# Strassen FFN on one core: the sums of G's blocks on GpSimd instead of DVE

## The chip, the cores and the metric

One core of a Trainium2 chip runs the whole kernel. The metric is the device time in microseconds (us), the median over runs. The core has TensorE (PE, matrix products), ScalarE (ACT), VectorE (DVE), GpSimd (POOL) and SyncE (SP), which issues all DMAs of this kernel.

## The reference

A low-rank mixture layer, then a linear layer whose output is masked, then a residual. `x` is 8 x 256 x 1024, 2048 tokens in all.

```python
# first layer: base + low-rank part, 8 experts of rank 16, top 2 by a router
base = x @ W.T                                       # 1024 x 1024
gates = softmax over the top 2 of (x @ Wr.T + language bias)
y = base + 2 * einsum(x @ A.T, gates, B)
# second layer, masked by hits of a softmax over 64 centroids
dots = softmax(y @ centroids.T / 0.1)
hits = dots > 0.01
query_sel, cluster_sel = any(hits, axis=1), any(hits, axis=0)
out = where(query_sel & cluster_sel[assignments], y @ weight.T + bias, 0)
return x + out
```

## The kernel before

The two linear layers have nothing nonlinear between them, so the kernel first makes G = W' V' (the product of both weights, and of W with the centroids), and then multiplies x by G, with the low-rank part added. Every matrix product is made in three passes over a high and a low part of each operand (`three`, L925): ScalarE copies a tile to the rounded type (`copy`, L393), and DVE subtracts that from the tile to get the low part (`rest`, L581).

**First sweep** (about 10 to 58 us): nine products of a weight block with half of V and the centroids, `m` = 0 to 8. ScalarE evicts each to `gop_raw` or `gb3_raw` and to the centroid columns.

**Second sweep** (about 58 to 187 us): for each pair of token tiles `n` = 0 to 7 TensorE does, in this order: `chunk(n, 0)`, half of the rest of G's row block n; `token_product(0, n)`, the tokens with the low-rank A, the router and the centroids; for `n >= 1` `turn_hg(n - 1)`, which turns the gated low-rank values; `chunk(n, 1)`; `lora_logits(n - 1)`, the low-rank part of the centroid logits, which waits for `hgt_lo` (semaphore `hgt_split`); `token_product(1, n)`. The last two chunks (`chunk(KD, 0)` and `chunk(KD, 1)`) follow.

**Product stage** (from 187 us): x times G, by a Strassen-like scheme. G is cut in 2 x 2 half-size blocks. `gop_raw` has seven slots: R11, R21, R22 (three blocks as they are) and T1 to T4, sums of them. The evictions write R11, R21, R22 and, into slot T3, the block R12. For each of four row blocks `jj`, and for each of the two column ranges (A1 = 224 columns from the first sweep, 288 from the second), four subtractions make T1 = R12 - R11, T3 = R22 - R12 (in place), T2 = R22 - T1 and T4 = T2 - R21. This is `t_sums` (L601), on DVE, eight calls: `k` = 0 to 3 in the first sweep after `m` = 2, 4, 6, 8; `k` = 4, 5, 6 in the second sweep at `n` = 2, 4, 6; `k` = 7 behind the loop over the pairs. Each waits for the eviction of the last block it reads (`g_evicted`); the calls at `n` = 2, 4, 6 and the last one read what `evict(n - 1, 1)` wrote, that is the evictions of n = 1, 3, 5, 7. Within a call T3 and T2 wait for T1, and T4 waits for both, over `t_step`; the last subtraction signals `t_made`.

Who reads the sums: `r_part` (L412) on ScalarE copies the three R slots and waits for the eviction only. `r_rest` (L612) on DVE writes the low part of the R slots into the same memory as their raw values, so it waits for `t_made` and for `r_part`. `t_part` (L417) on ScalarE copies all four T slots of a row block, and waits for `t_made`; `t_rest` (L617) on DVE follows it.

DVE's order is written out by hand. For a pair n in the second sweep (L739 to L752): `split_x(0, n)`, `route(n - 1)`; then for even n `t_sums` and `r_rest`, for odd n >= 3 `t_rest`; then `split_x(1, n)` (`xt_lo`), `split_hgt(n - 1)` (`hgt_lo`), `split_w`, and the softmax of the logits. GpSimd makes five constants at the start and has nothing else to do; it issues no DMA.

Of the kernel before, what the change touches and what calls it, by code (L numbers as in the profile page):

```python
# [5 lines left out]
ALU = mybir.AluOpType  # L6
# [9 lines left out]
HALF = 512  # L16
# [9 lines left out]
KD = D // P  # L26
KO = O // P
KG = KD + 1
KH = KD // 2
# [4 lines left out]
A1 = (HALF - C) // 2  # L34
# [5 lines left out]
R11, R21, R22, T1, T2, T3, T4 = range(7)  # L40
# [12 lines left out]
def adaln_ffn_kernel(nc, x, xt, ids, w9, awt, v1, v2, bias, assign, out):  # L53
# [9 lines left out]
    with ExitStack() as ctx:  # L63
# [3 lines left out]
        def sb_split(name, shape, stack=ctx):  # L67

            with nc.sbuf_tensor(name + "_raw", shape, F32) as raw:
                pass  # L70
            return raw, sb(name + "_lo", shape, F32R, stack)

        def sem(name):
            return ctx.enter_context(nc.semaphore(name))
# [39 lines left out]
        gop_raw, gop_lo = sb_split("gop", [P, 7, KH, HALF])  # L114
# [84 lines left out]
        g_evicted = sem("g_evicted")  # L199
        cent_split = sem("cent_split")  # L200
        t_step = sem("t_step")
        t_made = sem("t_made")
# [63 lines left out]
        def chunk_number(n, c):  # L266
            return KG + 2 * n + c + 1
# [103 lines left out]
        def _(pool):  # L371
# [7 lines left out]
                           allow_small_or_imprecise_dtypes=True).then_inc(const_ready, 1)  # L379
            nc.gpsimd.memset(ones_b[:], 1.0).then_inc(const_ready, 1)  # L380

        def raw_of(kb, cols):

            at = slice(R11, T3 + 1, T3) if kb % 2 == 0 else slice(R21, R22 + 1)
            return gop_raw[:, at, kb // 2, cols]
# [192 lines left out]
        def _(dve):  # L578
            def rest(dst, src, hi):

                return nc.vector.tensor_tensor(dst, src, hi.bitcast(F32), ALU.subtract)  # L581

            def minus(dst, a, b):
                return nc.vector.tensor_tensor(dst, a, b, ALU.subtract)

            def split_w(q):
                b = q % 2
                dve.wait_ge(w_hi_done, q + 1)
                rest(w_lo[b][:], (wraw if q <= KG else w_in_place)[b][:], w_hi[b][:]).then_inc(w_split, 1)
# [6 lines left out]
            def split_v2(p):  # L596
                dve.wait_ge(v2_hi, p + 1)
                j = slice(JP * p, JP * p + JP)
                rest(vt2_lo[:, j, :], vt2_raw[:, j, :], vt2_hi[:, j, :]).then_inc(v2_split, 1)

            def t_sums(k, jj, cols, number):  # L601

                g = gop_raw[:, :, jj, cols]
                dve.wait_ge(g_evicted, number)
                minus(g[:, T1, :], g[:, T3, :], g[:, R11, :]).then_inc(t_step, 1)
                dve.wait_ge(t_step, 3 * k + 1)
                minus(g[:, T3, :], g[:, R22, :], g[:, T3, :]).then_inc(t_step, 1)
                minus(g[:, T2, :], g[:, R22, :], g[:, T1, :]).then_inc(t_step, 1)
                dve.wait_ge(t_step, 3 * k + 3)
                minus(g[:, T4, :], g[:, T2, :], g[:, R21, :]).then_inc(t_made, 1)  # L610

            def r_rest(k, jj, cols):  # L612
                dve.wait_ge(t_made, k + 1)
                dve.wait_ge(r_hi, k + 1)
                rest(gop_lo[:, 0:3, jj, cols], gop_raw[:, 0:3, jj, cols], gop_hi_r[:, :, jj, cols]).then_inc(gop_split, 1)

            def t_rest(jj):  # L617
                dve.wait_ge(t_hi, jj + 1)
                rest(gop_lo[:, T1:T4 + 1, jj, :], gop_raw[:, T1:T4 + 1, jj, :], gop_hi_t[:, :, jj, :]).then_inc(gop_split, 1)
# [12 lines left out]
            def split_x(c, n):  # L632
                dve.wait_ge(xt_hi_done[c], n + 1)
                rest(xt_lo[c][:], xt_raw[c][:], xt_hi[c][:]).then_inc(xt_split[c], 1)

            def set_up():
                dve.wait_ge(const_ready, 5)
                dve.wait_ge(ids_landed, 16)
                dve.wait_ge(assign_landed, 16)
                nc.vector.memset(hit_sum[:], 0.0).then_inc(setup_step, 1)  # L640
                nc.vector.tensor_tensor(lang_bias[:], ids_raw[:].unsqueeze(2).broadcast_to([P, NB, E]),
                                        iota8[:].unsqueeze(1).broadcast_to([P, NB, E]),
                                        ALU.is_equal).then_inc(setup_step, 1)

                nc.vector.tensor_scalar(as_neg[:], as_raw[:], 0.0, float(C), ALU.is_lt, ALU.mult).then_inc(setup_step, 1)
                dve.wait_ge(setup_step, 3)
                nc.vector.tensor_scalar(lang_bias[:], lang_bias[:], LANG_BIAS, None, ALU.mult).then_inc(setup_step, 1)
                nc.vector.tensor_tensor(as_neg[:], as_raw[:], as_neg[:], ALU.add).then_inc(setup_step, 1)
                dve.wait_ge(setup_step, 5)
                nc.vector.tensor_scalar(as_neg[:], as_neg[:], 0.0, float(C - 1), ALU.max, ALU.min).then_inc(setup_step, 1)  # L650
                dve.wait_ge(setup_step, 6)
                nc.vector.tensor_scalar(onehot_a[:], as_neg[:], pidx[0:C, :], None, ALU.is_equal).then_inc(setup_step, 1)

            for m in range(KG):
                if m == KD:
                    split_x(0, 0)
                    split_x(1, 0)
                else:
                    split_w(m + 2)
                dve.wait_ge(g_evicted, m + 1)  # L660
                cent = ps[:, BANK_G[(m + 1) % 2], 2 * A1:HALF]
                if m == 0:
                    rest(gb_lo[:], cent, gb_hi[:]).then_inc(cent_split, 1)
                else:
                    rest(aw_lo[:, m - 1, AW:AWG], cent, aw_hi[:, m - 1, AW:AWG]).then_inc(cent_split, 1)
                if 2 <= m < 2 + PIECES:
                    split_v2(m - 2)
                if m == 6:
                    dve.wait_ge(awt_hi, 1)
                    rest(aw_lo[:, :, 0:AW], awt_raw[:], aw_hi[:, :, 0:AW]).then_inc(awt_split, 1)  # L670
                if m == 7:
                    set_up()
                if m == KD:
                    split_w(m + 2)
                if m >= 2 and m % 2 == 0:
                    t_sums(m // 2 - 1, m // 2 - 1, slice(0, A1), m + 1)
                    r_rest(m // 2 - 1, m // 2 - 1, slice(0, A1))

            def route(n):
# [36 lines left out]
            def split_hgt(n):  # L716
                dve.wait_ge(hgt_hi_done, n + 1)
                rest(hgt_lo[:], hgt_all[:, 2 * n * P:(2 * n + 2) * P], hgt_hi[:]).then_inc(hgt_split, 1)

            def softmax_max(n):  # L720
                base = SOFT_STEPS * n
                dve.wait_ge(logits_ready, n + 1)
                nc.vector.tensor_reduce(mx[:], ps_aw(n)[:, :, AW:AWG], AX_X, ALU.max).then_inc(soft, 1)
                dve.wait_ge(soft, base + 1)
                nc.vector.tensor_scalar(negb[:], mx[:], -1.0 / TEMPERATURE, None, ALU.mult).then_inc(soft, 1)

            def softmax_hits(n):
                base = SOFT_STEPS * n
                dve.wait_ge(exp_done, 2 * n + 2)
                nc.vector.reciprocal(rsum[:], esum[:]).then_inc(soft, 1)  # L730
                dve.wait_ge(soft, base + 3)
                for c in range(2):
                    nc.vector.tensor_scalar(hits[:, c, :], ex[:, c, :], rsum[:, c:c + 1], THRESHOLD,
                                            ALU.mult, ALU.is_gt).then_inc(soft, 1)
                dve.wait_ge(soft, base + 5)
                nc.vector.tensor_reduce(qsel[:, 2 * n:2 * n + 2], hits[:], AX_X, ALU.max).then_inc(soft, 1)
                nc.vector.tensor_tensor(hit_sum[:], hit_sum[:], hits[:], ALU.add).then_inc(soft, 1)

            for n in range(1, NPAIR):  # L739
                split_x(0, n)  # L740
                route(n - 1)
                jj = n // 2 - 1
                if n >= 2 and n % 2 == 0:
                    t_sums(KH + jj, jj, slice(A1, HALF), chunk_number(n - 1, 1))
                    r_rest(KH + jj, jj, slice(A1, HALF))
                elif n >= 2:
                    t_rest(jj)
                split_x(1, n)
                split_hgt(n - 1)
                split_w(n + KG + 1)  # L750
                softmax_max(n - 1)
                softmax_hits(n - 1)  # L752
# [33 lines left out]
                rest(hgm_lo[i % 2][:], hgt_all[:, 2 * i * P:(2 * i + 2) * P], hgm_hi[i % 2][:]).then_inc(hgm_split, 1)  # L786


            t_sums(2 * KH - 1, KH - 1, slice(A1, HALF), chunk_number(KD - 1, 1))
            r_rest(2 * KH - 1, KH - 1, slice(A1, HALF))  # L790
            rest_a(0)
            s_sums(0)
# [358 lines left out]
```

## Time and profile before

| | us |
|---|---|
| median of 3 runs | 376.43 (374.96 to 377.31) |
| the profiled execution | 375.24 |
| its span, first to last instruction | 373.1 |
| mean granted TensorE clock in it | 0.975 of full |

Times in the rows below are us from the start of the span, durations too unless marked ns. An engine's idle time before an instruction stands in brackets with what ended it. Two instructions of one engine overlap a little in the records, as the next one starts while the one before drains. The granted clock of 1.00 is TensorE's upper level, 2.4 GHz, and 0.50 its lower one, 1.2 GHz.

### The profile page before, as it was taken

What the parts mean: (1) busy time and instruction counts of PE and PEld (TensorE: products, weight loads), DVE (VectorE), ACT (ScalarE), POOL (GpSimd) and SP (SyncE); (2) the same over time, 40 slices, a digit from 0 to 9 for tenths busy, and PEclk for the clock granted to TensorE, in tenths of its full rate; (3) what the DMA queues carried; (4) which work ended last, traced back from release to release, by engine and by line L of the source; (5) the groups of instructions that cost most, each with busy time, mean ns of one, the idle gap of its engine ahead of it and who ended that gap; (6) DMA issues with size and microseconds to landing.
All of it is one profiled execution on the core that took longest, in us unless ns stands there. A gap on an engine that the chain in (4) does not pass through costs nothing.

```text
span 373.1 us, 4828 instructions
## 1 busy us (share of the span) xinstructions
PE 347.7 (93%) x1892; PEld 304.7 (82%) x1892; DVE 253.2 (68%) x439; ACT 133.7 (36%) x215; POOL 1.0 (0%) x9
## 2 busy tenths in 40 slices
PE   7899999998969897896997899999999999999993
PEld 6788889998969887896985588888888888888882
DVE  2627878456656647656766788985949598594936
ACT  4544563244433351454335142233213223321210
POOL 1000000000000000000000000000000000000000
PEclk9999999999987998998899999999999999999999
DMA  7667331433331332321380315272542707251202
GB/s 281 240 232 254 112 124 57 171 112 114 114 112 56 114 113 87 115 83 56 114 325 13 115 56 193 90 259 78 181 159 83 251 5 257 80 184 42 84 30 112
DMA packets 13782, 49.10 MB, mean 132 GB/s; under 512 B 1664, under 2 KB 1664, under 8 KB 13760
## 3 DMA queue, kind: packets, MB, share of 16 engines
q1 hardware_dynamic: 13760, 48.80, 36.3%
q8 instruction: 15, 0.25, 0.3%
q14 instruction: 7, 0.06, 0.1%
HBM read 40.41 MB, written 8.39 MB: 131 GB/s over the span
## 4 chain that ended last, share of the span: by engine, by line
PE 80%; DVE 9%; ACT 5%; DMA 4%; issue 1%; SPq 1%; DVEq 0%
PE ps L926 27%; PE ps L928 26%; PE ps L927 26%; DVE gop_lo L581 3%; DMA xt_raw<-in_xt 2%; DVE xt_lo L581 2%; DMA vt_raw<-in_v 2%; ACT gop_hi_t L393 1%; DVE hgt_lo L581 1%; ACT gop_hi_r L393 1%; ACT hgt_all L393 1%; ACT hgt_hi L393 0%; SPq L297 0%; PE ps L986 0%; ACT gb_hi L393 0%
## 5 line engine op out<-in xcount | busy, mean ns | idle before, releaser
L926 PE MATMUL ps<-vt_hi,w_hi 128*128 128x288 f32 (+1 forms) x216 | 71.5, 331 | 2.0 <-DVE vt_lo L581 2.0
L927 PE MATMUL ps<-vt_lo,w_hi 128*128 128x288 f32 (+1 forms) x216 | 70.5, 327 | 0.0
L928 PE MATMUL ps<-vt_hi,w_lo 128*128 128x288 f32 (+1 forms) x216 | 70.4, 326 | 0.0
L927 PE MATMUL ps<-gop_lo,sl_s_hi 128*128 128x512 f32 x128 | 49.8, 389 | 0.0
L393 ACT ACTIVATE u<-ps 128x512 f32<-128x512 f32 x32 | 19.1, 598 | 83.9 <-PE ps L928 54.2
L926 PEld LDWEIGHTS ps<-vt_hi,w_hi 128*128 128x128 f32 x216 | 40.8, 189 | 5.5 <-DVE vt_lo L581 1.6
L927 PEld LDWEIGHTS ps<-vt_lo,w_hi 128*128 128x128 f32 x216 | 40.7, 189 | 2.8
L928 PEld LDWEIGHTS ps<-vt_hi,w_lo 128*128 128x128 f32 x216 | 40.6, 188 | 2.9
L926 PE MATMUL ps<-aw_hi,xt_hi 128*128 128x200 f32 x128 | 38.6, 301 | 0.1
L927 PE MATMUL ps<-aw_lo,xt_hi 128*128 128x200 f32 x128 | 38.2, 298 | 0.0
L928 PE MATMUL ps<-aw_hi,xt_lo 128*128 128x200 f32 x128 | 38.0, 297 | 0.0
L926 PE MATMUL ps<-gop_hi_t,sl_s_hi 128*128 128x512 f32 x96 | 37.5, 391 | 0.0
L928 PE MATMUL ps<-gop_hi_t,sl_s_lo 128*128 128x512 f32 x96 | 37.4, 389 | 0.0
L819 DVE TENSOR_TENSOR u<-ps,u 128x512 f32<-128x512 f32 x8 | 5.5, 690 | 34.5 <-ACT u L393 34.5
L927 PEld LDWEIGHTS ps<-gop_lo,sl_s_hi 128*128 128x128 f32 x128 | 24.0, 188 | 4.9
L926 PEld LDWEIGHTS ps<-aw_hi,xt_hi 128*128 128x128 f32 x128 | 27.5, 215 | 0.3 <-issue 0.3
L928 PEld LDWEIGHTS ps<-aw_hi,xt_lo 128*128 128x128 f32 x128 | 27.6, 216 | 0.0
L927 PEld LDWEIGHTS ps<-aw_lo,xt_hi 128*128 128x128 f32 x128 | 27.6, 215 | 0.0
L581 DVE TENSOR_TENSOR w_lo<-wraw,w_hi 128x1024 fp32r<-128x1024 f32 (+1 forms) x11 | 12.4, 1128 | 19.5 <-ACT w_hi L393 19.2
L926 PE MATMUL ps<-gop_hi_r,sl_a_hi 128*128 128x512 f32 x64 | 25.0, 391 | 0.0
L927 PE MATMUL ps<-gop_lo,sl_a_hi 128*128 128x512 f32 x64 | 24.9, 389 | 0.0
L928 PE MATMUL ps<-gop_hi_r,sl_a_lo 128*128 128x512 f32 x64 | 24.9, 389 | 0.0
(123 smaller groups left out, 640.9 us busy)
## 6 DMA issues: line engine op xcount, KB each, us to landing
xt_raw<-in_xt SPq DMA_DIRECT2D x32, 512.0 KB, 3.7
nat<-in_x SPq DMA_DIRECT2D x16, 512.0 KB, 4.3
out<-nat SPq DMA_DIRECT2D x15, 512.0 KB, 2.7
wraw<-in_w SPq DMA_DIRECT2D x9, 512.0 KB, 3.3
w_raw<-in_w SPq DMA_DIRECT2D x8, 512.0 KB, 3.1
vt_raw<-in_v SPq DMA_DIRECT2D x4, 576.0 KB, 4.3
vt_raw<-in_v SPq DMA_DIRECT2D x4, 512.0 KB, 6.3
awt_raw<-in_awt SPq DMA_DIRECT2D x1, 544.0 KB, 6.1
```

What stands on the lines that cost most here:

```text
L393: return nc.scalar.activation(dst, src, ACT.Copy)
L581: return nc.vector.tensor_tensor(dst, src, hi.bitcast(F32), ALU.subtract)
L819: nc.vector.tensor_tensor(u[:, 3, :], bank(i, BANK_X), u[:, 3, :], ALU.add).then_inc(sum22, 1)
L926: nc.tensor.matmul(dst, l_hi, r_hi, start=start, stop=False, skip_group_check=True)
L927: nc.tensor.matmul(dst, l_hi, r_lo, start=False, stop=False, skip_group_check=True)
L928: return nc.tensor.matmul(dst, l_lo, r_hi, start=False, stop=stop, skip_group_check=True)
```

## The change

The eight calls of `t_sums` move from DVE's program to GpSimd's, where they stand in one row behind the constants, in the same order. Each keeps its wait for the eviction and its inner waits, now on GpSimd. The subtractions are `nc.gpsimd.tensor_tensor` in place of `nc.vector.tensor_tensor`, with the same operands. `r_rest` and `t_part` keep their waits for `t_made`, which now comes from GpSimd. Nothing else moves.

```diff
--- before.py
+++ after.py
@@ -379,6 +379,25 @@
                            allow_small_or_imprecise_dtypes=True).then_inc(const_ready, 1)
             nc.gpsimd.memset(ones_b[:], 1.0).then_inc(const_ready, 1)
 
+            def minus(dst, a, b):
+                return nc.gpsimd.tensor_tensor(dst, a, b, ALU.subtract)
+
+            def t_sums(k, jj, cols, number):
+
+                g = gop_raw[:, :, jj, cols]
+                pool.wait_ge(g_evicted, number)
+                minus(g[:, T1, :], g[:, T3, :], g[:, R11, :]).then_inc(t_step, 1)
+                pool.wait_ge(t_step, 3 * k + 1)
+                minus(g[:, T3, :], g[:, R22, :], g[:, T3, :]).then_inc(t_step, 1)
+                minus(g[:, T2, :], g[:, R22, :], g[:, T1, :]).then_inc(t_step, 1)
+                pool.wait_ge(t_step, 3 * k + 3)
+                minus(g[:, T4, :], g[:, T2, :], g[:, R21, :]).then_inc(t_made, 1)
+
+            for jj in range(KH):
+                t_sums(jj, jj, slice(0, A1), 2 * jj + 3)
+            for jj in range(KH):
+                t_sums(KH + jj, jj, slice(A1, HALF), chunk_number(2 * jj + 1, 1))
+
         def raw_of(kb, cols):
 
             at = slice(R11, T3 + 1, T3) if kb % 2 == 0 else slice(R21, R22 + 1)
@@ -597,17 +616,6 @@
                 dve.wait_ge(v2_hi, p + 1)
                 j = slice(JP * p, JP * p + JP)
                 rest(vt2_lo[:, j, :], vt2_raw[:, j, :], vt2_hi[:, j, :]).then_inc(v2_split, 1)
-
-            def t_sums(k, jj, cols, number):
-
-                g = gop_raw[:, :, jj, cols]
-                dve.wait_ge(g_evicted, number)
-                minus(g[:, T1, :], g[:, T3, :], g[:, R11, :]).then_inc(t_step, 1)
-                dve.wait_ge(t_step, 3 * k + 1)
-                minus(g[:, T3, :], g[:, R22, :], g[:, T3, :]).then_inc(t_step, 1)
-                minus(g[:, T2, :], g[:, R22, :], g[:, T1, :]).then_inc(t_step, 1)
-                dve.wait_ge(t_step, 3 * k + 3)
-                minus(g[:, T4, :], g[:, T2, :], g[:, R21, :]).then_inc(t_made, 1)
 
             def r_rest(k, jj, cols):
                 dve.wait_ge(t_made, k + 1)
@@ -673,7 +681,6 @@
                 if m == KD:
                     split_w(m + 2)
                 if m >= 2 and m % 2 == 0:
-                    t_sums(m // 2 - 1, m // 2 - 1, slice(0, A1), m + 1)
                     r_rest(m // 2 - 1, m // 2 - 1, slice(0, A1))
 
             def route(n):
@@ -741,7 +748,6 @@
                 route(n - 1)
                 jj = n // 2 - 1
                 if n >= 2 and n % 2 == 0:
-                    t_sums(KH + jj, jj, slice(A1, HALF), chunk_number(n - 1, 1))
                     r_rest(KH + jj, jj, slice(A1, HALF))
                 elif n >= 2:
                     t_rest(jj)
@@ -786,7 +792,6 @@
                 rest(hgm_lo[i % 2][:], hgt_all[:, 2 * i * P:(2 * i + 2) * P], hgm_hi[i % 2][:]).then_inc(hgm_split, 1)
 
 
-            t_sums(2 * KH - 1, KH - 1, slice(A1, HALF), chunk_number(KD - 1, 1))
             r_rest(2 * KH - 1, KH - 1, slice(A1, HALF))
             rest_a(0)
             s_sums(0)
```

## Rows read from the trace of the kernel before

**Rows 1.** The busy table, from the page: us, share of the span, instructions.

```profile
PE 347.7 (93%) x1892; PEld 304.7 (82%) x1892; DVE 253.2 (68%) x439; ACT 133.7 (36%) x215; POOL 1.0 (0%) x9
```

**Rows 2.** What TensorE waited for: total us, times, longest.

```profile
PE ps L926 <- DVE hgt_lo L581: 12.5, 6, 3.2
PE ps L926 <- DVE vt_lo L581: 2.0, 2, 1.2
```

**Rows 3.** TensorE in order of time, second sweep: start, duration, instruction, [idle before, releaser].

```profile
93.26 0.30 PE L926 MATMUL ps<-gb_hi,hgt_hi 128*128 128x64 f32 x1 [1.00 <-DVE hgt_lo L581]
...
109.27 0.42 PE L926 MATMUL ps<-gb_hi,hgt_hi 128*128 128x64 f32 x1 [3.15 <-DVE hgt_lo L581]
```

**Rows 4.** DVE's groups by shape: name, count | busy us, mean ns | idle before.

```profile
L584 DVE TENSOR_TENSOR gop_raw<-gop_raw 128x288 f32<-128x288 f32 x16 | 6.9, 454 | 0.3
L584 DVE TENSOR_TENSOR gop_raw<-gop_raw 128x224 f32<-128x224 f32 x16 | 5.9, 388 | 0.3
```

**Rows 5.** DVE in order of time, first sweep.

```profile
28.46 1.36 DVE L581 TENSOR_TENSOR vt_lo<-vt_raw,vt_hi 128x1152 fp32r<-128x1152 f32 x1 [0.24 <-ACT vt_hi L393]
29.73 1.54 DVE L584 TENSOR_TENSOR gop_raw<-gop_raw 128x224 f32<-128x224 f32 x4
...
32.30 1.23 DVE L581 TENSOR_TENSOR w_lo<-wraw,w_hi 128x1024 fp32r<-128x1024 f32 x1
...
33.90 1.36 DVE L581 TENSOR_TENSOR vt_lo<-vt_raw,vt_hi 128x1152 fp32r<-128x1152 f32 x1 [0.23 <-ACT vt_hi L393]
```

**Rows 6.** DVE and then ScalarE in order of time, pair 2; DVE of pair 4.

```profile
86.17 1.80 DVE L584 TENSOR_TENSOR gop_raw<-gop_raw 128x288 f32<-128x288 f32 x4
...
90.68 1.06 DVE L581 TENSOR_TENSOR gop_lo<-gop_raw,gop_hi_r 128x864 fp32r<-128x864 f32 x1 [2.70 <-ACT gop_hi_r L393]
...
123.60 1.06 DVE L581 TENSOR_TENSOR gop_lo<-gop_raw,gop_hi_r 128x864 fp32r<-128x864 f32 x1 [3.31 <-ACT gop_hi_r L393]
...
89.10 0.39 ACT L393 ACTIVATE hgt_all<-ps 128x256 f32<-128x256 f32 x1 [0.58 <-PE ps L986]
```

**Rows 7.** DVE and then ScalarE in order of time, around the last call.

```profile
177.49 1.80 DVE L584 TENSOR_TENSOR gop_raw<-gop_raw 128x288 f32<-128x288 f32 x4
...
183.82 0.69 DVE L765 TENSOR_TENSOR s_raw<-xt_raw 128x512 f32<-128x512 f32 x1 [2.29 <-DMA xt_raw<-in_xt]
...
179.32 1.91 ACT L393 ACTIVATE gop_hi_t<-gop_raw 128x2048 fp32r<-128x2048 f32 x1 [1.17 <-DVE gop_raw L584]
```

**Rows 8.** GpSimd in order of time, its constants.

```profile
1.17 0.29 POOL L374 TENSOR_SCALAR_AFFINE_SELECT ident<-ident 128x128 f32<-128x128 f32 x1 [0.23 <-POOL ident L372]
1.42 0.14 POOL L376 IOTA iota<- 128x8 f32 x1
```

**Rows 9.** ScalarE's evictions of chunk(3, 1) and chunk(7, 1), in order of time.

```profile
106.15 0.41 ACT L393 ACTIVATE gop_raw<-ps 128x288 f32<-128x288 f32 x1 [0.73 <-PE ps L928]
...
170.57 0.41 ACT L393 ACTIVATE gop_raw<-ps 128x288 f32<-128x288 f32 x1 [0.74 <-PE ps L928]
```

**Rows 10.** DVE in order of time, at the odd pairs 3 and 7.

```profile
105.45 2.29 DVE L581 TENSOR_TENSOR gop_lo<-gop_raw,gop_hi_t 128x2048 fp32r<-128x2048 f32 x1 [5.23 <-ACT gop_hi_t L393]
107.66 1.22 DVE L581 TENSOR_TENSOR xt_lo<-xt_raw,xt_hi 128x1024 fp32r<-128x1024 f32 x1
108.79 0.42 DVE L581 TENSOR_TENSOR hgt_lo<-hgt_all,hgt_hi 128x256 fp32r<-128x256 f32 x1
...
169.87 2.29 DVE L581 TENSOR_TENSOR gop_lo<-gop_raw,gop_hi_t 128x2048 fp32r<-128x2048 f32 x1 [5.24 <-ACT gop_hi_t L393]
```

**Rows 11.** Busy us (instructions) of each engine in four stretches, clock, DMA.

```profile
108.90:115.70 6.80, 6.43 (x30) 6.44 (x31) 4.11 (x10) 1.65 (x5) 0.00 (x0) 0.50 0.00 0
143.00:146.40 3.40, 3.40 (x18) 3.40 (x18) 2.53 (x9) 1.65 (x5) 0.00 (x0) 0.51 0.03 5
173.80:180.60 6.80, 6.80 (x32) 6.80 (x33) 5.42 (x14) 3.74 (x7) 0.00 (x0) 0.50 0.00 0
116.00:119.00 3.00, 3.00 (x25) 3.00 (x24) 2.65 (x17) 0.20 (x1) 0.00 (x0) 1.00 0.48 175
```

## The prediction, made before the change was run

> **What bounds the kernel now.** I read the busy table first: TensorE works for 347.7 of the 373.1 us, DVE for 253.2, and GpSimd for 1.0, all of that in its constants at the start [rows 1]. Anything that doesn't make TensorE wait, or run at its low clock, is free. The list of TensorE's waits comes next: its largest entry is 12.5 us in six waits for one DVE tile, `hgt_lo` [rows 2]. Placed in time these are two kinds, all in the second sweep. Before the LoRA logits of an even pair (2, 4, 6) TensorE idles 1.00 us, before those of an odd pair (3, 5, 7) 3.15 us; one row of each kind is shown, there are three of each [rows 3]. So the question is what the edit does to the DVE queue in front of `hgt_lo` at those six places, and whether it makes a seventh.
>
> **What is taken off DVE.** Eight calls of `t_sums`, four subtractions each: 16 of 128x224 at 388 ns and 16 of 128x288 at 454 ns, 5.9 + 6.9 = 12.8 us [rows 4]. How much of it stands in front of a wait of TensorE?
>
> - First sweep, four calls (after blocks 2, 4, 6, 8). The call of block 2 runs from 29.73 to 31.27, then `r_rest`, then the low part of W from 32.30 [rows 5]. Behind it is nothing of TensorE's: the six waits for `hgt_lo` lie in the second sweep, and the next entry, for `vt_lo`, 2.0 us in two [rows 2], is from the first products at the start; none lies between 16 and 92 us. A weight block lasts 5.44 us here (the low part of V at 28.46 and again at 33.90), and the W part of 32.30 is for the block after next. Worth 0.
> - Second sweep, pairs 2, 4, 6. The sums of pair 2 run from 86.17 to 87.97; then DVE sits idle 2.70 us until ScalarE has delivered `gop_hi_r`, and only then do `r_rest`, `xt_lo` and `hgt_lo` follow [rows 6]. Without the sums DVE idles 1.8 us more. The 1.00 us stalls stay. Worth 0.
> - The last call, 177.49 to 179.29. ScalarE's copy of the T blocks had waited 1.17 us for it, and `r_rest` follows it on DVE, but DVE's next sums wait 2.29 us for a DMA until 183.82 [rows 7]. The four operations end inside that gap with or without 1.8 us of sums ahead. Worth 0.
>
> So the relief is 12.8 us of DVE time and 0 us of path. If one of these covers were missing, the most that could come back is one call, 1.8 us.
>
> **What is put on GpSimd.** 32 subtractions. No row shows that engine subtracting. Nearest rows: a one-input select over 128 elements takes 0.29 us and an iota of 8 takes 0.14 [rows 8], so 0.15 us for 120 elements, 1.25 ns each on 0.14. For 288 elements that is 0.50 us if the second input is free, and 0.14 + 0.72 = 0.86 if it costs as much as the first. I take 0.68. The same select idled 0.23 us for the semaphore of the memset before it [rows 8]; a call has two such inner waits. A call alone then lasts 4 x 0.68 + 2 x 0.23 = 3.2 us (2.5 to 3.9). The skill's "GPSIMD Engine Reference", Performance versus the Vector engine, gives 4497 ns for a two-input float32 operation over 2048 elements; scaled down, an estimate of 0.63 us, and a sum of 3.0 us in place of 3.2.
>
> Nobody needs that result soon. The sums for pair 4 can start when the eviction that begins at 106.15 is over, about 106.56 [rows 9]; their reader, `r_rest` of pair 4, runs at 123.60 [rows 6], 17 us later. The tightest is the last call: its eviction begins at 170.57 [rows 9], so it may run from about 171; `r_rest` and the low part of A, 1.06 + 1.22 us, would fit before the DMA lands at 183.82 if it ended by 181.5. That is 10 us for 3.2.
>
> No DMA moves. The queue that the sums join has only the constants ahead of them. The new wait that matters is `r_rest`'s, on `t_made` from another engine: behind it on DVE stand `xt_lo`, `hgt_lo` and the next W.
>
> **Where the sums now run.** This decides. GpSimd doesn't wait for its place in DVE's order; it starts at the eviction. For the sums of pairs 4, 6 and the last call the eviction is that of pairs 3, 5 and 7, and it falls exactly under the three 3.15 us stalls. The order there: DVE starts `gop_lo` (2.29 us) at 105.45, the eviction ends at about 106.56, `xt_lo` starts at 107.66 and `hgt_lo` at 108.79, and TensorE is released at 109.27; the third place, from 169.87 with the eviction of 170.57, is the same to 0.01 us, and so is the one between [rows 3, 9, 10]. All three DVE operations read two SBUF tensors, as do GpSimd's. Every us that GpSimd's reads take from DVE between 106.56 and 109.2 is a us of the whole kernel.
>
> No row shows both engines at work together, so I bound it. Nothing shared: 0. All four sums in front of `hgt_lo`: 4 x 0.68 = 2.7 us a place (3.4 at the price of 0.86). I take the middle, strict turns: `gop_lo` finishes, one sum, `xt_lo`, one sum, `hgt_lo`: 2 x 0.68 = 1.4 us a place, three places, **4.2 us**. A slowdown spread over the same stretch instead of turns gives much the same, as about half a call fits in it. The skill's "SBUF — State Buffer", Who interferes with whom, says that a DVE instruction with two SBUF inputs contends with a GpSimd instruction that reads SBUF, and that the second to come is blocked until the first ends. By that rule the price is the one of turns; a reader can't test it on the trace before, since GpSimd is idle there from 2 us on.
>
> The even places see less: pair 2's sums start after the eviction of pair 1 (about 80 us). If they held DVE for a whole 2.7 us, the last operation of `route`, behind which the sums start at 86.17, would end near 88.9, where ScalarE gets the turned result of it at 89.10 after TensorE's two transposes [rows 6]. That is 0.4 us at worst; I take 0. In the first sweep the sums push DVE about 1 us later under covers of some 5. I take 0.
>
> **The clock.** After each odd stall the granted clock is at its lower level, 1.2 GHz: 0.50 over 6.80 us, 0.51 over 3.40 us, 0.50 over 6.80 us [rows 11]. TensorE issues 32 matmuls in 6.80 us there against 25 in 3.00 us at the full level, so 3.40 us of it cost about 1.7 us. A stall of 4.55 instead of 3.15 us can change these stretches. The first begins during the wait already, so more of it may pass while TensorE idles (gives back up to 0.7, half of 1.4), and likewise the third; the second, the short one, may grow to the size of the others (costs 1.7). -0.7 - 0.7 + 1.7 = +0.3: I take 0 and keep 3.4 each way (two stretches of that size changed) for the range.
>
> **Sum.** -0 (DVE's relief) + 4.2 (turns at three stalls) + 0 (clock) = +4.2 us. The profiled execution took 375.24 (its span of 373.1 and 2.1 around it), 1.2 below the median of the runs, 376.43. So 379.4 for such an execution, and 376.4 + 4.2 = 380.6 for the median.
>
> **Rivals.**
> 1. *Nothing is shared, or DVE keeps its turn.* DVE's operations follow each other without a gap from 105.45 to 109.2 [rows 10], so a DVE that never lets go starves GpSimd until the gap behind, which the 10 to 17 us of cover allow. Then 0 on the path: 376.4. This is the other side of my forecast. It decides if less than 0.4 us a place is lost. For it: no row shows any cost. Against: no row shows two engines reading two SBUF tensors each at no cost either, and this kernel has no such pair before the change.
> 2. *More than two sums a place.* Three (T3 and T2 are issued back to back) or four: 6.1 to 8.2 us, 382.5 to 384.6, with a longer clock stretch up to 386 or 388.
> 3. *Sums so slow that they are waited for.* `t_made` would have to come after 181.5, that is 2.6 us a subtraction; three times my upper price. Then the start of the product stage slips by what is beyond.
> 4. *A gain.* One mechanism: the shift moves the clock's stretches and two long ones come out short, -3.4 us, 373.0 with nothing lost to sharing. Not below -1%.
>
> **How the numbers follow.** Turns, with one or two sums a place: 0.45; nothing shared: 0.32; more: 0.17; slow sums or something else slower: 0.02; a gain: 0.04. The likeliest is turns with two, 380.6; its own range is 378 to 384. The range reaches down to the case of nothing shared less half the spread of the runs, 375.5, and up into the second rival, 386. A measurement here can tell about 1%, 3.8 us. The 4.2 lies just above that, so turns split about 0.28 slower and 0.17 within 1%; nothing shared goes within; rival 2 slower. Together faster 0.04, same 0.49, slower 0.47.
>
> **What would show it.** The waits for `hgt_lo` at the odd places: 3.15 us means that nothing is shared, 4.5 turns, 5.9 and more rival 2; the even ones stay at 1.00. `xt_lo` (1.22 us) and `hgt_lo` (0.42 us) under the sums would be longer or start with a gap. GpSimd's subtractions of 288: 0.5 to 0.9 us. DVE's busy time should fall by 12.8 us to about 240. No new wait of TensorE for anything of the T blocks; one would prove the slack wrong. A different length of the clock's low stretches with unchanged stalls would show the time moved by the clock alone.

## The result and the profile after

| | before | after |
|---|---|---|
| median, us | 375.87 (374.96 to 377.31, 4 runs) | 381.50 (380.58 to 382.89, 4 runs) |
| ratio, 95% interval | | 1.0149 [1.0102, 1.0196] |
| the profiled execution | 375.24 | 381.56 |
| its span | 373.1 | 379.5 |

Slower by 5.6 us, 1.5%; the interval of the ratio makes that 3.8 to 7.4 us. The ratios leave out executions in a slower state, in the tables here one of e1 (692.55 us), one of e2 (1940.65) and two of the kernel before beside e1 to e4. The busy table after, against [rows 1]; then what TensorE waited for (us in total, times, longest), against [rows 2]:

```profile
PE 350.1 (92%) x1892; PEld 307.0 (81%) x1892; DVE 248.3 (65%) x407; ACT 133.8 (35%) x215; POOL 40.2 (11%) x41
```

```profile
PE ps L931 <- DVE hgt_lo L600: 16.0, 6, 4.3
...
PE ps L991 <- DVE hg L718: 0.9, 1, 0.9
```

DVE has 32 instructions fewer (407 for 439) and GpSimd 32 more, but DVE lost only 4.9 us of busy time instead of 12.8: something lengthened its other work by 7.9. The waits for `hgt_lo` grew from 12.5 to 16.0 us in the same six. TensorE in order of time, the first matmul behind each of the six, after:

```profile
94.07 0.30 PE L931 MATMUL ps<-gb_hi,hgt_hi 128*128 128x64 f32 x1 [1.00 <-DVE hgt_lo L600]
...
111.27 0.42 PE L931 MATMUL ps<-gb_hi,hgt_hi 128*128 128x64 f32 x1 [4.34 <-DVE hgt_lo L600]
...
128.97 0.30 PE L931 MATMUL ps<-gb_hi,hgt_hi 128*128 128x64 f32 x1 [1.00 <-DVE hgt_lo L600]
...
146.16 0.30 PE L931 MATMUL ps<-gb_hi,hgt_hi 128*128 128x64 f32 x1 [4.34 <-DVE hgt_lo L600]
...
163.24 0.30 PE L931 MATMUL ps<-gb_hi,hgt_hi 128*128 128x64 f32 x1 [1.00 <-DVE hgt_lo L600]
...
180.43 0.30 PE L931 MATMUL ps<-gb_hi,hgt_hi 128*128 128x64 f32 x1 [4.34 <-DVE hgt_lo L600]
```

and the four of before that [rows 3] leaves out:

```profile
126.18 0.30 PE L926 MATMUL ps<-gb_hi,hgt_hi 128*128 128x64 f32 x1 [1.00 <-DVE hgt_lo L581]
...
142.19 0.30 PE L926 MATMUL ps<-gb_hi,hgt_hi 128*128 128x64 f32 x1 [3.15 <-DVE hgt_lo L581]
...
157.67 0.30 PE L926 MATMUL ps<-gb_hi,hgt_hi 128*128 128x64 f32 x1 [1.00 <-DVE hgt_lo L581]
...
173.68 0.38 PE L926 MATMUL ps<-gb_hi,hgt_hi 128*128 128x64 f32 x1 [3.15 <-DVE hgt_lo L581]
```

The even stalls are the same 1.00 us. The three odd ones went from 3.15 to 4.34: 3 x 1.19 = 3.6 us. What fills them (DVE, then GpSimd, pair 3 and the last call), against [rows 10]:

```profile
106.26 2.29 DVE L600 TENSOR_TENSOR gop_lo<-gop_raw,gop_hi_t 128x2048 fp32r<-128x2048 f32 x1 [5.22 <-ACT gop_hi_t L412]
108.47 1.81 DVE L600 TENSOR_TENSOR xt_lo<-xt_raw,xt_hi 128x1024 fp32r<-128x1024 f32 x1
110.20 1.01 DVE L600 TENSOR_TENSOR hgt_lo<-hgt_all,hgt_hi 128x256 fp32r<-128x256 f32 x1
111.14 1.81 DVE L600 TENSOR_TENSOR w_lo<-w_raw,w_hi 128x1024 fp32r<-128x1024 f32 x1
...
107.45 1.75 POOL L383 TENSOR_TENSOR gop_raw<-gop_raw 128x288 f32<-128x288 f32 x1 [23.11 <-ACT gop_raw L412]
...
109.28 1.65 POOL L383 TENSOR_TENSOR gop_raw<-gop_raw 128x288 f32<-128x288 f32 x1
...
110.89 0.97 POOL L383 TENSOR_TENSOR gop_raw<-gop_raw 128x288 f32<-128x288 f32 x1
```

`gop_lo` keeps its 2.29 us. `xt_lo` takes 1.81 us instead of 1.22 and `hgt_lo` 1.01 instead of 0.42: 0.59 more each, with no gap between them. GpSimd's first subtraction starts under `gop_lo` and lasts 1.75 us, where the same operation lasts 0.805 us with DVE on other work (around 81 us, pair 1's sums, 3.34 us for the four of them):

```profile
81.00 3.34 POOL L383 TENSOR_TENSOR gop_raw<-gop_raw 128x288 f32<-128x288 f32 x4 [15.33 <-ACT gop_raw L412]
107.45 6.15 POOL L383 TENSOR_TENSOR gop_raw<-gop_raw 128x288 f32<-128x288 f32 x4 [23.11 <-ACT gop_raw L412]
142.35 6.14 POOL L383 TENSOR_TENSOR gop_raw<-gop_raw 128x288 f32<-128x288 f32 x4 [28.75 <-ACT gop_raw L412]
176.62 6.15 POOL L383 TENSOR_TENSOR gop_raw<-gop_raw 128x288 f32<-128x288 f32 x4 [28.12 <-ACT gop_raw L412]
```

The first subtraction ends 0.65 us behind `gop_lo` (109.20 against 108.55), the second 0.65 behind `xt_lo`: the rest of their 0.805 us passed before. So each engine stands still while the other reads, and the standing time is booked as busy.

The rest is TensorE's clock. Windows over the stretches at the lower level (the columns of [rows 11]; the two numbers behind GpSimd's are clock and DMA share):

```profile
109.20:119.40 10.20, 8.13 (x37) 8.13 (x38) 7.76 (x22) 1.85 (x6) 4.24 (x3) 0.50 0.09 24
146.80:153.60 6.80, 6.80 (x32) 6.80 (x32) 4.90 (x19) 1.85 (x6) 1.66 (x1) 0.50 0.05 10
180.60:187.70 7.10, 7.10 (x35) 7.10 (x36) 5.42 (x10) 4.26 (x7) 2.09 (x2) 0.52 0.00 0
```

Before, the three lasted 6.80, 3.40 and 6.80 us, 16.6 of it with TensorE at work [rows 11]. Now they last 10.20, 6.80 and 7.10, with 22.0 at work. 5.4 us more at half rate is 2.7. The positions above say when it was lost. Against before, the six matmuls come +0.81, +2.00, +2.79, +3.97, +5.57 and +6.75 us later, and the end +6.4. The odd stalls hold three steps of 1.19. Between them lie +0.79 and +1.60, together +2.4 for the clock. That is the difference of these two executions; how much of it belongs to the change is taken up with the prediction's clock term below. Behind the last one 0.4 comes back: the wait for `hg` is 0.9 us here and was 1.3. Of the +0.81, 0.66 is there at 27 us (DVE's `w_lo` starts at 27.52 for 26.86); TensorE's waits for `vt_lo` in the first 12 us, which hang on the first loads, were 2.6 us here and 2.0 before. The other 0.15 stands at the first token product:

```profile
62.45 0.33 PE L931 MATMUL ps<-aw_hi,xt_hi 128*128 128x200 f32 x1 [0.26 <-DVE aw_lo L600]
```

This matmul started at 61.63 before, with no such wait. DVE had waited for GpSimd's third call in the first sweep and was late from there on. All five kernels with the first sweep's sums on GpSimd (the change, e1, e2, e5, e7) have this wait, the others don't: a small cost of the change that the prediction put at 0.

### The profile page after: what moved, and what is told of

Its sections match the earlier page's. It is cut to its first block, busy times and chain, and to the rows that moved or that the text cites. A ratio compares the mean times of both kernels' runs of the same rounds, so it can differ in the third digit from the quotient of the medians.

```text
span 379.5 us, 4828 instructions
## 1 busy us (share of the span) xinstructions
PE 350.1 (92%) x1892; PEld 307.0 (81%) x1892; DVE 248.3 (65%) x407; ACT 133.8 (35%) x215; POOL 40.2 (11%) x41
## 4 chain that ended last, share of the span: by engine, by line
PE 76%; DVE 12%; ACT 5%; DMA 4%; issue 2%; POOL 1%; SPq 1%; DVEq 0%
PE ps L931 25%; PE ps L933 25%; PE ps L932 25%; DVE gop_lo L600 3%; DVE xt_lo L600 3%; DMA xt_raw<-in_xt 2%; DMA vt_raw<-in_v 2%; ACT gop_hi_t L412 1%; DVE hgt_lo L600 1%; POOL gop_raw L383 1%; ACT gop_hi_r L412 1%; ACT hgt_all L412 1%; ACT hgt_hi L412 0%; SPq L297 0%; PE ps L991 0%
## 5 line engine op out<-in xcount | busy, mean ns | idle before, releaser
L931 PE MATMUL ps<-vt_hi,w_hi 128*128 128x288 f32 (+1 forms) x216 | 72.4, 335 | 2.6 <-DVE vt_lo L600 2.6
L383 POOL TENSOR_TENSOR gop_raw<-gop_raw 128x224 f32<-128x224 f32 (+1 forms) x32 | 39.2, 1234 | 141.8 <-ACT gop_raw L412 95.3
L931 PEld LDWEIGHTS ps<-vt_hi,w_hi 128*128 128x128 f32 x216 | 41.6, 193 | 6.2 <-DVE vt_lo L600 2.0
L932 PEld LDWEIGHTS ps<-vt_lo,w_hi 128*128 128x128 f32 x216 | 41.5, 192 | 2.8
L600 DVE TENSOR_TENSOR xt_lo<-xt_raw,xt_hi 128x1024 fp32r<-128x1024 f32 x16 | 21.2, 1329 | 6.3 <-ACT xt_hi L412 6.3
```

The costliest lines, as they stand in the source:

```text
L383: return nc.gpsimd.tensor_tensor(dst, a, b, ALU.subtract)
L931: nc.tensor.matmul(dst, l_hi, r_hi, start=start, stop=False, skip_group_check=True)
L932: nc.tensor.matmul(dst, l_hi, r_lo, start=False, stop=False, skip_group_check=True)
```

## The experiments

Each ran against the kernel before on the same chip; the ratios are to that, and the stalls are those of one profiled execution each. The theory is the one of the prediction: GpSimd and DVE take turns at reading, and only what stands between the eviction and `hgt_lo` at the odd pairs costs.

| run | odd stalls, us | median, us | before, us | ratio [95%] |
|---|---|---|---|---|
| the change | 4.34 | 381.50 | 375.87 | 1.0149 [1.0102, 1.0196] |
| e1, sums behind `hgt_lo` | 3.15 | 376.26 | 375.03 | 1.0002 [0.9964, 1.0040] |
| e2, only the first sweep's | 3.15 | 375.02 | 375.03 | 0.9985 [0.9950, 1.0019] |
| e3, four unread subtractions | 3.98 | 380.05 | 375.03 | 1.0123 [1.0070, 1.0176] |
| e4, twelve unread memsets | 3.15 | 375.71 | 375.03 | 1.0016 [0.9974, 1.0059] |
| e5, halves | 3.74 | 378.93 | 375.16 | 1.0084 [1.0054, 1.0113] |
| e8, one-input operations | 3.55 | 377.19 | 374.59 | 1.0077 [1.0034, 1.0120] |
| e9, one subtraction | 3.57 | 377.60 | 374.59 | 1.0068 [1.0033, 1.0102] |
| e6, before reordered | none | 354.26 | 375.16 | 0.9447 [0.9389, 0.9504] |
| e7, changed reordered | none | 357.70 | 375.16 | 0.9524 [0.9468, 0.9581] |

**e1: the same sums on GpSimd, later.**

```diff
             for jj in range(KH):
+                pool.wait_ge(hgt_split, 2 * jj + 1)
                 t_sums(KH + jj, jj, slice(A1, HALF), chunk_number(2 * jj + 1, 1))
```

> The changed kernel, with one more wait on GpSimd: each of the four calls behind the first sweep waits until hgt_lo of the pair in which its eviction falls is written. The same sums, on the same engine, only later. Turns theory (GpSimd's reads block xt_lo and hgt_lo): the three odd stalls of TensorE for hgt_lo are back at 3.15 us (4.34 in the changed kernel), and the time is that of the kernel before, 375.9, within 1 us; what DVE loses then lies in w_lo and the softmax, which are covered. Rival (a slower or later t_made, or GpSimd doing this work at all, is what costs): 381.5 or more, since t_made comes still later.

Measured: no difference from before. DVE and then GpSimd in order of time, pair 3:

```profile
110.29 1.22 DVE L601 TENSOR_TENSOR xt_lo<-xt_raw,xt_hi 128x1024 fp32r<-128x1024 f32 x1
111.43 0.42 DVE L601 TENSOR_TENSOR hgt_lo<-hgt_all,hgt_hi 128x256 fp32r<-128x256 f32 x1
...
111.93 4.22 POOL L383 TENSOR_TENSOR gop_raw<-gop_raw 128x288 f32<-128x288 f32 x4 [25.68 <-DVE hgt_lo L601]
```

`xt_lo` and `hgt_lo` are back at 1.22 and 0.42. GpSimd starts at 111.93, later than in the change, `t_made` comes later still, and it costs nothing that these runs can tell (the interval is 1.5 us each way, and 0.15 us of the wait for `aw_lo` would hide in it). That GpSimd does the work is next to free; its place is what is paid for. The four of 4.22 us here were also stretched by DVE (one of them 1.71 us), under cover.

**e2: only the first sweep's four calls on GpSimd.**

```diff
             for jj in range(KH):
                 t_sums(jj, jj, slice(0, A1), 2 * jj + 3)
-            for jj in range(KH):
-                t_sums(KH + jj, jj, slice(A1, HALF), chunk_number(2 * jj + 1, 1))
```

(and on DVE, `t_sums` and its calls behind the first sweep as before)

> The changed kernel, with only the four calls of the first sweep on GpSimd, the other four back on DVE. Turns theory: those four run under no stall, so 375.9 to 376.3 (0.3 for the one late aw_lo at the start of the second sweep); the hgt_lo stalls are 3.15 and 1.00. Rival (the cost is spread over all calls, 5.6 us over eight): 378.7.

Measured: the same time as before, -0.15% with an interval that holds 0. DVE waits for GpSimd there, up to 1.9 us a call in the changed kernel and 6.4 in all (6.3 in e2), of which only the 0.26 us at `aw_lo` reaches TensorE:

```profile
DVE gop_lo L600 <- POOL gop_raw L383: 6.4, 4, 1.9
```

**e3 and e4: the kernel before, with work on GpSimd that nobody reads.**

```diff
+            for n in (3, 5, 7):
+                pool.wait_ge(g_evicted, chunk_number(n, 1))
+                for _ in range(4):           # e4: range(12)
+                    nc.gpsimd.tensor_tensor(spare[:], spare[:], spare[:], ALU.subtract).then_inc(spare_done, 1)
+                    # e4: nc.gpsimd.memset(spare[:], 0.0).then_inc(spare_done, 1)
+                    done += 1
+                    pool.wait_ge(spare_done, done)
```

> The kernel before, its sums on DVE, and beside it work on GpSimd that nobody reads: after the evictions of chunk(n, 1), n = 3, 5, 7, four subtractions of a spare tile of 128x256 from itself. It adds work and leaves none out. Turns theory: two of them get in front of hgt_lo, each for 0.59 x 256/288 = 0.53 us; stalls 3.15 + 1.05 = 4.2, three of them, 3.2 us, and the clock's share of up to 2.5: 379 to 381.6. Rival (what costs is the dependence on GpSimd's results): 375.9, stalls 3.15.

> As the run with the unread subtractions, but twelve memsets of the spare tile at each place, which read nothing and keep GpSimd going for about as long. If only reads are shared: stalls 3.15, 375.9, xt_lo 1.22 and hgt_lo 0.42 us. Rival (anything GpSimd does slows DVE, through its writes, its semaphores or its power): stalls above 3.4 us and 377 or more.

Measured: the unread subtractions make the kernel before slower by 1.2%, as the change does by 1.5%; the memsets do nothing. DVE in order of time, e3 and then e4:

```profile
108.48 1.64 DVE L592 TENSOR_TENSOR xt_lo<-xt_raw,xt_hi 128x1024 fp32r<-128x1024 f32 x1
110.04 0.83 DVE L592 TENSOR_TENSOR hgt_lo<-hgt_all,hgt_hi 128x256 fp32r<-128x256 f32 x1
```

```profile
108.72 1.22 DVE L592 TENSOR_TENSOR xt_lo<-xt_raw,xt_hi 128x1024 fp32r<-128x1024 f32 x1
109.85 0.42 DVE L592 TENSOR_TENSOR hgt_lo<-hgt_all,hgt_hi 128x256 fp32r<-128x256 f32 x1
...
107.75 4.37 POOL L389 MEMSET spare<- 128x256 f32 x12 [105.72 <-ACT gop_raw L404]
```

In e3 0.42 us each instead of the 0.53 expected: the two inputs were the same tile of 256 columns. In e4 GpSimd is at work through the whole stretch (twelve in 4.37 us) and `xt_lo` and `hgt_lo` have not moved. So it is GpSimd's reads, and neither the moved work, nor its semaphores, nor GpSimd's activity as such.

**e5: each subtraction behind the first sweep in two halves.**

```diff
-                minus(g[:, T1, :], g[:, T3, :], g[:, R11, :]).then_inc(t_step, 1)
+                for h in g:                      # the two halves of 144 columns
+                    minus(h[:, T1, :], h[:, T3, :], h[:, R11, :]).then_inc(t_step, 1)
```

(T3, T2 and T4 likewise, and the waits count the doubled signals)

> The changed kernel, with each subtraction of 288 columns behind the first sweep cut into two of 144, in the same order on GpSimd. Turns theory: still two instructions get in front of hgt_lo, but half as long, so each lengthens a DVE operation by 0.3 instead of 0.59 us: stalls 3.15 + 0.6 = 3.75, and 375.9 + 1.8 + 0 to 2 for the clock = 377.7 to 379.7. Rival (both engines share a rate, and DVE is slowed as long as GpSimd reads): the stretch holds as much reading as before, stalls 4.3, 381.5.

Measured: stalls 3.74, time +0.84%. DVE, pair 3:

```profile
110.95 1.51 DVE L616 TENSOR_TENSOR xt_lo<-xt_raw,xt_hi 128x1024 fp32r<-128x1024 f32 x1
112.38 0.70 DVE L616 TENSOR_TENSOR hgt_lo<-hgt_all,hgt_hi 128x256 fp32r<-128x256 f32 x1
```

0.29 and 0.28 us more, half of 0.59, with the same amount of reading queued on GpSimd. That tells turns from a shared rate: DVE loses one GpSimd instruction's read for each of its own instructions, however much is waiting.

**e8 and e9: the unread work with one input, and with one subtraction only.**

```diff
-                    nc.gpsimd.tensor_tensor(spare[:], spare[:], spare[:], ALU.subtract).then_inc(spare_done, 1)
+                    nc.gpsimd.tensor_scalar(spare[:], spare[:], 1.0, None, ALU.mult).then_inc(spare_done, 1)
```

```diff
-                for _ in range(4):
+                for _ in range(1):
```

> As the run with four unread subtractions at each odd place, but each operation reads the spare tile once (times 1.0) instead of twice. If a read of GpSimd holds DVE's second input for the whole instruction, whatever it reads: DVE operations are lengthened by the length of this shorter operation, some 0.3 us, and as the operations are shorter up to three get in front of hgt_lo: stalls 3.5 to 4.0, 376.5 to 379. Rival (only a second input of GpSimd gets into DVE's way): stalls 3.15, 375.

> As the run with four unread subtractions at each odd place, but one at each. Turns theory: the one gets its turn between gop_lo and xt_lo, so xt_lo is lengthened by 0.53 and hgt_lo stays at 0.42: stalls 3.15 + 0.5 = 3.65, 375 + 1.6 + 0 to 1.5 for the clock = 376.6 to 378. Rival (DVE pays only when GpSimd has several instructions queued, or finishes first): stalls 3.15.

Measured, DVE in order of time at pair 3, e8 and then e9:

```profile
107.38 1.42 DVE L592 TENSOR_TENSOR xt_lo<-xt_raw,xt_hi 128x1024 fp32r<-128x1024 f32 x1
108.72 0.61 DVE L592 TENSOR_TENSOR hgt_lo<-hgt_all,hgt_hi 128x256 fp32r<-128x256 f32 x1
```

```profile
110.20 1.64 DVE L592 TENSOR_TENSOR xt_lo<-xt_raw,xt_hi 128x1024 fp32r<-128x1024 f32 x1
111.76 0.41 DVE L592 TENSOR_TENSOR hgt_lo<-hgt_all,hgt_hi 128x256 fp32r<-128x256 f32 x1
```

A one-input operation costs 0.20 us a turn, half of the two-input one of the same width (0.42), and two of them get in front of `hgt_lo`, not the three that I had allowed for. The stalls of 3.55 lie in my range by luck: I had expected a shorter operation that blocks DVE for the whole of its length. On GpSimd it is the longer one, 0.85 us against 0.67 (the shortest of twelve each). The first of them:

```profile
106.46 1.72 POOL L389 TENSOR_SCALAR spare<-spare 128x256 f32<-128x256 f32 x1 [104.44 <-ACT gop_raw L404]
```

It ends at 108.18, 0.72 us behind `gop_lo` (107.46), and yet `xt_lo` is lengthened by 0.20 only. So DVE waits for the reads and not for the end of GpSimd's instruction. One subtraction costs `xt_lo` 0.42 and leaves `hgt_lo` at 0.41. The time went up by more than the stalls: 3 x 0.4 = 1.2 us of stalls against 0.77% and 0.68%, 2.9 and 2.5 us. For one kernel alone that is not clear of noise (the intervals are 1.3 to 4.5 and 1.2 to 3.8 us), but e3, e5 and the change lean the same way. The difference goes with the clock: span times (1 - mean clock), averaged over the runs that the ratios count, is 11.2 us in e8 and 11.1 in e9 (12.7 with one run listed at a clock of 0.928, though it was the fastest) against 9.1 in before beside them; 12.2 in e3 and 11.5 in e5 against 9.6 and 9.4; 13.0 in the change; but 9.9 in e1, 9.7 in e4 and 9.0 in e2 against 9.6. This measure counts TensorE's idle time at the lower level too, so it overstates the price.

**e6 and e7: what the stalls themselves hang on.** Both orders of `xt_lo` and `hgt_lo` against the G work were tried, on DVE alone and with GpSimd:

```diff
+                split_x(1, n)
+                split_hgt(n - 1)
                 if n >= 2 and n % 2 == 0:
                     t_sums(...)          # in e6 only
                     r_rest(KH + jj, jj, slice(A1, HALF))
                 elif n >= 2:
                     t_rest(jj)
-                split_x(1, n)
-                split_hgt(n - 1)
                 split_w(n + KG + 1)
```

> The kernel before, with xt_lo and hgt_lo ahead of the sums, r_rest and t_rest in DVE's order of a pair. If the six stalls are only due to these two standing behind the low parts of G's blocks: xt_lo and hgt_lo are done at 104.0, ahead of TensorE's 106.1; all six stalls go, 12.5 us, and with them the stretches at the lower clock, 16.7 us at half rate, 8.3 us: about 355. Rival (something else is late next, r_rest and t_rest at the start of the product stage, or the W blocks): less than 6 us gained, 370.

> The changed kernel with the same reordering. Turns theory: xt_lo and hgt_lo are over before the eviction that lets GpSimd start, so what GpSimd takes from DVE is covered; same time as the reordered kernel before within 1 us, about 355. Rival (GpSimd's sums cost wherever they stand): 5 us more than that one.

Measured: e6 is 5.5% faster than before, at 354.3, a version that beats both kernels. In the profiled execution TensorE has no wait for `hgt_lo` and none at all between 11 and 176 us, and no stretch at the lower clock but in the last 2.5 us of the span, behind its last matmul. e7 is 3.4 us slower than e6, where I expected them to be equal; their four runs each don't overlap. TensorE's waits, e6 and then e7:

```profile
PE ps L926 <- DVE vt_lo L581: 1.9, 2, 1.0
...
PE ps L986 <- DVE hg L711: 0.8, 1, 0.8
```

```profile
PE ps L931 <- DVE vt_lo L600: 3.1, 2, 2.3
PE ps L991 <- DVE hg L718: 1.6, 1, 1.6
...
PE ps L931 <- DVE xt_lo L600: 1.5, 2, 0.8
```

DVE of e7 behind the eviction of pair 3 (left out here: four small operations):

```profile
105.39 2.29 DVE L600 TENSOR_TENSOR gop_lo<-gop_raw,gop_hi_t 128x2048 fp32r<-128x2048 f32 x1 [1.37 <-ACT gop_hi_t L412]
107.60 1.83 DVE L600 TENSOR_TENSOR w_lo<-w_raw,w_hi 128x1024 fp32r<-128x1024 f32 x1
...
109.66 0.45 DVE L732 TENSOR_SCALAR negb<-mx 128x2 f32<-128x2 f32 x1
...
111.07 0.88 DVE L740 TENSOR_SCALAR hits<-ex,rsum 128x64 f32<-128x64 f32 x2
...
112.39 1.22 DVE L600 TENSOR_TENSOR xt_lo<-xt_raw,xt_hi 128x1024 fp32r<-128x1024 f32 x1
...
106.58 5.15 POOL L383 TENSOR_TENSOR gop_raw<-gop_raw 128x288 f32<-128x288 f32 x4 [21.85 <-ACT gop_raw L412]
```

The expected order came true: `hgt_lo` is over at 104.0, ahead of the sums. What I had wrong is that the rest is covered. GpSimd's four subtractions fall on `w_lo` (1.83 instead of 1.22), `negb` and `hits`, and in that stretch DVE has hardly a gap left: from `gop_lo` to the next `xt_lo` it takes 7.00 us, in e6 5.66. So `xt_lo` of the next pair comes late, twice, for 0.76 us each: 1.5 us in waits that e6 doesn't have, and 0.26 at `aw_lo`. The rest of the 3.4 stays open. The wait for `hg` is 0.8 longer, but it is 0.8 us in e1 and 1.6 in e9 too, whatever the sums do, and the 1.2 at `vt_lo` hangs on the first loads. The rival for e7, that the sums cost wherever they stand, is wrong as a rule (e1, e2) but in part right in this kernel, where the stalls that had been cover were gone.

## Why the prediction was right, and where its sizes were off

- **DVE's relief is worth 0.** Right. e2 puts four of the calls on GpSimd and e1 all eight, and neither is faster than before (the intervals leave room for 1.9 and 1.4 us).
- **The path: sums of pairs 4, 6 and the last call start under the odd stalls.** Right, place and mechanism: GpSimd's starts at 107.45, 142.35 and 176.62, the even stalls at 1.00, turns with two sums in front of `hgt_lo`. Rival 1 (nothing shared) had 0.32; e3 against e4 excludes it. The spread-out slowdown, which the prediction priced like turns, is excluded by e5. Rival 2 (more than two) doesn't happen even where the sums are shorter (e5, e8).
- **The price of a turn.** Mis-sized. I took the whole of GpSimd's operation, 0.68 us. The operation is 0.805 us alone (in my 0.50 to 0.86), but DVE pays only 0.59 of it: 0.59, 0.42, 0.29 and 0.20 us for two inputs of 288, of 256 (one tile twice), of 144, and one input of 256 columns. 3 x 2 x 0.59 = 3.6 instead of 4.2. The Trainium skill's "SBUF — State Buffer", Who interferes with whom, beside which the turns were put, is borne out in who blocks whom, also in that a GpSimd instruction which only writes blocks nobody (e4). Its wait until the first ends is longer than what these rows show: 0.59 us of 0.805 in the change, and in e8 0.20 us where GpSimd's instruction goes on for 0.72 us after DVE has let it in. The estimate of 0.63 us from the Trainium skill's "GPSIMD Engine Reference", Performance versus the Vector engine, was low by 0.17.
- **The clock, taken as 0.** The term furthest off. I let the first and third stretch give back 0.7 each, since TensorE would idle in them. In the profiled execution the first grew from 6.80 to 10.20 us instead, the second from 3.40 to 6.80 as I had feared, the third from 6.80 to 7.10: +2.4 us between the stalls, within the 3.4 that I kept for the range. But these stretches differ between executions without any change of the stalls, and one pair of them doesn't tell what the change costs. e4 has the stalls of before, and its second stretch is 6.80 us long too; e3 has longer stalls, and its first is 3.40 (busy us of each engine, clock, DMA):

```profile
143.25:150.05 6.80, 6.80 (x34) 6.80 (x34) 4.11 (x15) 1.68 (x6) 1.21 (x4) 0.50 0.01 2
...
111.90:115.30 3.40, 3.40 (x18) 3.40 (x17) 2.53 (x9) 1.64 (x5) 0.99 (x1) 0.50 0.00 0
```

What can be said rests on the runs: 5.6 - 3.6 leaves 2.0 us in the medians, 0.15 of it at `aw_lo`, and the interval of the ratio allows 0.2 to 3.8. That it is the clock is supported by the measure under e9, and not shown by itself.
- **Slack behind the sums.** Right. The last call ends 6.15 us after 176.62, and `r_rest` waits for ScalarE's copy, not for GpSimd. In the first sweep DVE was late by less than the 1 us that I gave it (the W part behind the first call starts at 33.20 for 32.30, of which 0.7 is the later start of the whole), with up to 1.9 us of waiting for GpSimd a call, which I had not named. It was not quite free: 0.15 us at `aw_lo`, taken as 0.
- **DVE's busy time, about 240.** Wrong, 248.3: I had not seen that time spent blocked is booked as busy.

The sum, 380.6, came out 0.9 us low, closer than its terms deserve, which is in part luck: the price of a turn was 0.6 too high, the clock and `aw_lo` together 2.0 too low, and the median of before has come down from 376.43 to 375.87. (The lower end of the range was misadded too: 376.4 less half the spread of the runs is 375.2, not 375.5.) The mechanism was right and its place too. What the 1.5% can't tell is turns with one sum from turns with two; the rows do.

## What to carry to other kernels

Work moved to an idle engine isn't free because that engine is idle: ask when it will now start, and what the engine with which it shares a read path does at that moment. Here a wait that holds the moved work back until the critical pair of operations is over (e1) takes the cost away, within 1.5 us. And look at what stands in front of the operation that the bound engine waits for: moving two lines of DVE's order (e6) brought 21 us, where DVE's relief from the sums was worth nothing.

## What the runs showed of the hardware

- GpSimd's subtractions hold up one-input DVE operations too. In the change, `negb` (128x2) takes 0.44 instead of 0.17 us under the sums, and one of the `hits` operations of pair 1 is longer by about 0.45; `mx`, which reads PSUM, is not (0.28). No run here has memsets beside them. The DVE timeline of the change:

```profile
112.87 0.28 DVE L730 TENSOR_REDUCE mx<-ps 128x2 f32<-128x128 f32 x1
113.18 0.44 DVE L732 TENSOR_SCALAR negb<-mx 128x2 f32<-128x2 f32 x1
```

- A float32 subtraction on GpSimd takes 0.805 us over 288 columns, 0.497 over 144 when undisturbed, so about 2.1 ns a column on 0.19 us, and 0.672 over 256 with one tile read twice; DVE's is 0.454 us over 288.
- Longer waits of TensorE came with more time than their length in all five kernels that have them: 1.2 us of added stalls with 2.5 to 2.9 (e8, e9), 1.8 with 3.2 (e5), 2.5 with 4.6 (e3), 3.6 with 5.6 (the change). Each interval reaches down to about the length of the stalls. Which stretch at the lower clock grows, and by how much, differs between executions and stays open.
